# First maxima moved into and behind the projection stage, weights loaded by columns, first y block loaded in halves

## Chip, cores and metric

One core of a Trainium2 chip runs the whole program. The metric is the device time of one execution in microseconds (us), lower is better. The profile is of one further execution; its times are those of the core's own clock, and clock shares are of TensorE's full 2.4 GHz.

## What is computed

The input x is (2, 2048, 512). A conditioned transformer layer is followed by a second layer with a cumulative average. All arithmetic is float32; most products are made three times, with operands split into a high and a low part.

```python
scale, offset = t_emb @ w_scale, t_emb @ w_offset
h = layer_norm(x) * scale + offset
q, k, v = h @ wq / sqrt(512), h @ wk, h @ wv      # 16 heads of 32; q, k then get the rotary embedding
a = softmax(q @ k.T); x = x + (a @ v) @ wo        # 2048 x 2048 logits per batch and head
x = x + gelu(layer_norm(x, s) @ w1) @ w2
# second layer
att = exp((x @ aw - max over the sequence) * temperature)
attn_out = att * cumsum(x @ values) / (att * counts + 1e-30)
op = attn_out @ operator + vector
res = relu(concat([x, op]) @ ff1 + b1) @ ff2 + b2 + x
out = layer_norm(res) * gamma + beta
```

## The kernel before

The program is a chain of stages, each one block of five instruction streams (PE, DVE, ACT, POOL, SP) that wait for each other by semaphores. A stage ends when all its streams are done, and the next begins after its semaphores have been cleared. All results between stages go through DRAM. The order of work in every stream is written out by hand.

**Projection stage** (`prepare`, L81 to L429). Eight blocks n of 512 tokens, four per batch. SP loads x, the conditioning weights (`wa`, `wb`), the joint qkv weight in four chunks of 128 rows (`load_w`, L133) and the rotary table. DVE takes the mean and variance and makes `x_norm` (L282); PE turns it (`turn`, L188), ACT makes h and its high part (`affine`, L353 on), DVE the low part (L289). The qkv weight is split by ACT (L384) and DVE (L317) into a staging buffer of two slots. PE then makes per block eight projections of q and k (L215, 12 matmuls each) and four of v (L224). A q or k projection is rotated by DVE (L303, L305) and POOL (L424), split by ACT (L368) and POOL (L412) and stored by SP (L167), from buffers of four slots. Six PSUM banks go round among the projections. In block 1 there is a small product for the bias (L231, through `vectors`), from `ff1`.

**First maxima** (`first_maxima`, L784 to L911). The softmax needs the row maximum of each block of logits before its scores. For the first 16 row groups (4 heads by 4 groups of 128 queries), and for three groups of the next block, this stage makes them: 76 matmuls of 96 x 512 (L866), each reduced by DVE (L888); PE turns the collected maxima (L876), DVE copies them (L897), SP writes them as a row of the stacked queries (L830). SP first loads queries and keys head by head (`load_head`, L810 on), six DMAs for each of q and k. Beside this PE makes a product of two weights, `operator` by half of `ff1`, as 32 matmul steps (L851), which ACT copies (L906) and SP stores as `wp` (L834). POOL sets a row of ones (L910).

**Attention** (`attend`). 512 steps, 16 key blocks by 4 query blocks by 4 head groups by 2 batches. A step has four score matmuls (L577), four maxima matmuls of a later block (L603), exponentials (ACT, L725), and values (L625). The sum over keys is made by POOL (`POOL_ROUNDS`: step offset and key block added; pairs are first added by DMA, L758) and for key blocks 8 and 14 by PE (L636); `last_sums` (L644) waits for POOL's last round and ends on PE. ACT copies values (L732) and sums (L738), SP stores them.

**Feed-forward** (`feed_forward`). SP loads the sums of all of attention (L1070), DVE takes the reciprocal (L1332), SP stores it as `rl` (L1077). A block of 512 tokens is projected in four parts of 128 (`project`, L1163): SP loads y (L1042) and, as four broadcast DMAs, the reciprocals (L1045) into one buffer, POOL multiplies (L1386), ACT and DVE split (L1222, L1280), PE projects, DVE adds x and takes statistics (L1287, L1289). For the first block nothing else is there for PE; for later ones this is mixed into the up and down products. `load_y` of a part waits for the split of the part before.

**Average** (`average`) is not touched.

## Time and profile before

| | us |
|---|---|
| median of 3 runs (range) | 3707.03 (3705.38 to 3714.58) |
| the profiled execution's own time | 3699.31 |
| its span | 3697.5 |
| PE busy in the span | 3452.5 (93%) |
| mean granted clock | 0.966 |

The span is divided by stage: the first PE work on projections is at 43 us and the last ends at 336 us; the first maxima run from 343 to 422 us; attention from 425 to 2120 us; feed-forward from 2123 us; the average takes the last 600 us or so. A row of the timeline gives start and duration of a run of like instructions, engine, line, operation, output and inputs, how many, and in brackets the idle time before with what ended it. "SPq" and "POOLq" are DMA issues or the engine's sequencer.

### The profile page before, as it was taken

To read this page: it belongs to the slowest core of one execution; us is meant where nothing else is said; L and a number is where in the kernel's file an instruction comes from. 1 tells how busy PE (TensorE), PEld (TensorE's weight loads), DVE (VectorE), ACT (ScalarE), POOL (GpSimd) and SP (SyncE) were. 2 spreads that over 40 slices of the span, in tenths; PEclk is the share of its full clock that TensorE was granted. 3 is DMA by queue.
4 is the path that set the end of the run, shared out by engine and by line. 5 is a ranking of instruction groups with operands and counts; after the bars stand their busy time and mean duration, and the time that the engine had idled before them with its cause. 6 is when DMAs were issued, how large, how long until landed. Compare 5 with 4: busy or idle time off the path is not lost. (4 is left out here: it accounts for less than half of the span.)

```text
span 3697.5 us, 47212 instructions
## 1 busy us (share of the span) xinstructions
PE 3452.5 (93%) x16640; PEld 2256.5 (61%) x16640; DVE 2039.8 (55%) x3300; ACT 1517.4 (41%) x2793; POOL 2109.3 (57%) x1675
## 2 busy tenths in 40 slices
PE   7997899999999999999999759999999995999997
PEld 5775445555554545455455248888888874777776
DVE  5764777777777777777777134222222213434443
ACT  2332366666666666666666522111111112221121
POOL 2655188888988888788888812222222213544553
PEclk9998999999999999999999869999999997999999
DMA  5646686868777786967765443122222114212220
GB/s 184 186 147 183 124 150 120 156 132 153 145 129 148 136 145 120 153 136 136 146 126 109 102 129 105 54 80 66 72 72 69 58 38 144 78 61 79 73 77 37
DMA packets 178716, 421.23 MB, mean 114 GB/s; under 512 B 16176, under 2 KB 65840, under 8 KB 153392
## 3 DMA queue, kind: packets, MB, share of 16 engines
q1 hardware_dynamic: 155440, 250.44, 26.4%
q0 software_dynamic: 23040, 167.78, 23.5%
q8 instruction: 131, 2.15, 0.3%
q14 instruction: 105, 0.86, 0.1%
HBM read 163.10 MB, written 87.03 MB: 68 GB/s over the span
## 5 line engine op out<-in xcount | busy, mean ns | idle before, releaser
L682 DVE TENSOR_REDUCE part_max<-ps_att 128x1 f32<-128x512 f32 x1972 | 1226.1, 683 | 384.8 <-PE ps_att L603 384.6
L725 ACT ACTIVATE probs<-ps_att 128x512 f32<-128x512 f32 x2048 | 1063.4, 602 | 524.0 <-PE ps_att L577 461.6
L776 POOL TENSOR_TENSOR prob_sums<-prob_sums,probs 128x512 f32<-128x512 f32 x896 | 1162.8, 1579 | 43.3 <-DMA probs<-probs 43.3
L577 PE MATMUL ps_att<-q_stack,k_stack 97*128 97x512 f32 x2048 | 867.6, 427 | 30.4 <-ACT probs L725 24.1
L603 PE MATMUL ps_att<-k_stack,q_stack 96*128 96x512 f32 x1972 | 784.0, 398 | 0.0
L577 PEld LDWEIGHTS ps_att<-q_stack,k_stack 97*128 97x128 f32 x2048 | 388.6, 190 | 518.8 <-ACT probs L725 365.3
L625 PE MATMUL ps_att<-probs,v_tok 128*32 128x512 f32 x4096 | 549.3, 608 | 0.0
L1381 POOL TENSOR_TENSOR ff_g_lo<-ff_g,ff_g_hi 128x512 fp32r<-128x512 f32 x128 | 165.1, 1290 | 555.8 <-DVE ff_g_hi L1345 555.8
L603 PEld LDWEIGHTS ps_att<-k_stack,q_stack 96*128 96x128 f32 x1972 | 377.1, 191 | 68.2
L1251 ACT ACTIVATE ff_g<-ps_ff 128x512 f32<-128x512 f32 x128 | 76.6, 599 | 580.6 <-PE ps_ff L1135 580.6
L758 POOL DMA_DIRECT2D probs<-probs x160 | 153.5, 959 | 257.0 <-PE ps_att L625 242.1
L1815 POOL TENSOR_TENSOR av_gated_lo<-av_full,av_gated_hi 128x512 fp32r<-128x512 f32 x64 | 93.3, 1459 | 270.0 <-ACT av_gated_hi L1668 270.0
L1345 DVE CAST ff_g_hi<-ff_g 128x512 fp32r<-128x512 f32 x128 | 54.9, 429 | 304.3 <-ACT ff_g L1251 304.3
L776 POOL TENSOR_TENSOR prob_sums<-probs 128x512 f32<-128x512 f32 x128 | 165.4, 1448 | 47.6 <-DMA probs<-probs 47.6
L625 PEld LDWEIGHTS ps_att<-probs,v_tok 128*32 128x32 f32 x4096 | 80.8, 108 | 182.7 <-ACT probs L725 175.2
L424 POOL TENSOR_TENSOR rotated<-rot_a,rot_b 128x512 f32<-128x512 f32 x64 | 92.4, 1443 | 154.7 <-DVE rot_b L305 149.5
L1668 ACT ACTIVATE av_gated_hi<-av_full 128x512 fp32r<-128x512 f32 x64 | 40.5, 632 | 263.7 <-DVE av_full L1776 263.7
L1135 PE MATMUL ps_ff<-ff_h_hi,w_hi 128*128 128x512 f32 x512 | 143.3, 402 | 0.7 <-ACT ff_h_hi L1263 0.7
L1776 DVE TENSOR_TENSOR av_full<-ps_avg,av_gate_rows 128x512 f32<-128x512 f32 x64 | 44.2, 691 | 177.1 <-PE ps_avg L1562 139.0
L1150 PE MATMUL ps_ff<-w_hi,ff_g_hi 128*128 128x512 f32 x512 | 141.5, 398 | 0.0
L1135 PE MATMUL ps_ff<-ff_h_hi,w_lo 128*128 128x512 f32 x512 | 141.0, 397 | 0.0
L1135 PE MATMUL ps_ff<-ff_h_lo,w_hi 128*128 128x512 f32 x512 | 140.7, 396 | 0.0
(183 smaller groups left out, 4648.0 us busy)
## 6 DMA issues: line engine op xcount, KB each, us to landing
probs<-probs POOLq DMA_DIRECT2D x160, 1024.0 KB, 8.5
q_stack<-qk SPq DMA_DIRECT2D x186, 128.0 KB, 7.3
k_stack<-qk SPq DMA_DIRECT2D x42, 512.0 KB, 11.0
qk<-rot_hi SPq DMA_DIRECT2D x64, 256.0 KB, 4.1
qk<-rot_lo SPq DMA_DIRECT2D x64, 256.0 KB, 2.6
av_gate_rows<-gate SPq DMA_DIRECT2D x64, 256.0 KB
x_in_sb<-in_x SPq DMA_DIRECT2D x8, 1024.0 KB, 8.7
v<-v_stage SPq DMA_DIRECT2D x8, 1024.0 KB, 5.1
```

The source lines that it names most:

```text
L424: nc.gpsimd.tensor_tensor(rot[:, u % 2, :], ra[:, u % 2, :], rb[:, u % 2, :], ALU.add)\
L577: nc.tensor.matmul(sT[u % 3], t["kS"][0:S3 + 1, b, h, k * P:(k + 1) * P], t["qS"][0:S3 + 1, h, n * TB:(n + 1) * TB], start=True, stop=True)\
L603: nc.tensor.matmul(mx[mx_uses % 3], t["qS"][0:S3, h, n * TB + q * P:n * TB + (q + 1) * P], t["kS"][0:S3, b, h, k * TB:(k + 1) * TB], start ...
L625: mm = nc.tensor.matmul(o_ps[rows, :], t["v"][:, steps[w]["b"], k, rows], t["p"][:, w % PR, h, :], start=(k == 0), stop=(k == LT - 1))
L682: nc.vector.tensor_reduce(t["pm"][:, r, k:k + 1], mx[mx_uses % 3], AX.X, ALU.max)\
L725: nc.scalar.activation(t["p"][:, at % PR, h, :], sT[(at * G + h) % 3], ACT.Exp)\
L758: nc.gpsimd.dma_start(t["p"][:, w % PR], t["p"][:, (w + 1) % PR], accum_op=ALU.add).then_inc(sem, 16)
L776: nc.gpsimd.tensor_tensor(x, first, t["p"][:, w % PR, h, :], ALU.add).then_inc(s["acc_done"], 1)
L1135: mm = nc.tensor.matmul(ps[:, 4 + u % 2, :], w[:, f, m * P:(m + 1) * P], h[:, f, :], start=(i == 0 and f == 0), stop=(i == 2 and f == DC - 1))
L1150: mm = nc.tensor.matmul(ps[:, j, :], g[:, u % 2, j * P:(j + 1) * P], w[:, m, :], start=(m == 0 and i == 0), stop=(m == MC - 1 and i == 2))
L1381: nc.gpsimd.tensor_tensor(gl[:, u % 2, :], gf[:], gh[:, u % 2, :].bitcast(F32), ALU.subtract)\
L1815: nc.gpsimd.tensor_tensor(al[:, v % 2, :], af[:, v % 2, :], ah[:, v % 2, :].bitcast(F32), ALU.subtract).then_inc(s["a_lo"], 1)
```

## The change

Five edits, all in the four functions named:

1. The 76 maxima of `first_maxima` move into `prepare`. From block 5 (`MAX_FROM`) one maxima matmul follows each of the twelve projections of a block, 36 in all, with its reduction on DVE; the other 40 come behind the last projection, each with a step of the weight product while there are any. The maxima share the ring of six banks. Heads are loaded by SP among the stores of blocks 4 to 6, three DMAs of 32 rows each in place of six of 16. The bias product goes from block 1 to behind the last block. `first_maxima` is gone; queries 1 and 2 and the values of the first unit are now loaded at the start of attention, and the row of ones is set in two parts.
2. The qkv weight is loaded by columns (q, k, v) in three DMAs of 1 MB; the projections go through all q first, then k; x is normed in place; the loads of x move.
3. In the last block of attention PE adds key blocks 8, 11, 12, 13, 14, 15 and POOL five rounds in place of eight.
4. The reciprocals of batch 0 are made inside attention, those of batch 1 in block 0 of feed-forward (`AT_RECIP`).
5. The first block of y and its reciprocals come in two halves of 256 tokens into the idle buffers of h (`load_first`).

```diff
+LAST_SUMS = (8, 11, 12, 13, 14, 15)
+LAST_ROUNDS = tuple(x for x in POOL_ROUNDS if x[1] not in LAST_SUMS)
...
+MAX_FROM = 5
...
+        rh, rl = sb("rot_hi", [P, 4, TB]), sb("rot_lo", [P, 4, TB])
+        wa, wb = rh, rl
...
+        raw = vst[:].rearrange("p a g j n -> p a (g j n)").rearrange("p a (f n) -> p a f n", f=DC)
+        op = x[:].rearrange("p a j f -> p (a j f)").rearrange("p (k n) -> p k n", k=DC)
+        ff, q1 = hf, hl[:, 0, 0, :]
+        kept = vst[:, 0].rearrange("p g j n -> p (g j n)").rearrange("p (i n) -> p i n", i=4)
+        pieces = [(i, slice(i * D, (i + 1) * D), slice(f, f + 2), float(D) ** -0.5 if i == 0 else 1.0)
+                  for i in range(3) for f in (0, 2)]
...
-        uses = []
+        uses, early = [], 0
         for n in range(NA):
-            uses += [("qk", n * QK + i) for i in range(QK)] + [("v", n * TT + j) for j in range(TT)]
-            if n == 1:
-                uses += [("b1", 0)]
+            for kind, first, count in (("qk", n * QK, QK), ("v", n * TT, TT)):
+                for i in range(count):
+                    uses += [(kind, first + i)]
+                    if n >= MAX_FROM:
+                        uses += [("mx", early)]
+                        early += 1
+        uses += [("b1", 0)]
+        for m in range(early, TT * AHEAD):
+            uses += [("mx", m)]
+            if m == TT * JOBS + TT - 1:
+                uses += [("mt", 0)]
...
                 def load_x(n):
                     if n >= 2:
-                        sp.wait_ge(s["xn"], TT * (n - 1))
+                        sp.wait_ge(s["turned"], DC * (n - 1))
                     sp.dma_start(x[:, n % 2], x_v[n]).then_inc(s[f"x_in{n % 2}"], 16)
 
...
+                def load_w(i):
+                    if i >= 2:
+                        sp.wait_ge(s["w_lo"], 2 * (i - 1))
+                    sp.dma_start(raw[:, i % 2], a["wqkv"][:, :, i * D:(i + 1) * D]).then_inc(s[f"wq_in{i % 2}"], 16)
...
                 sp.dma_start(wb[:], a["w_offset"]).then_inc(s["w_in"], 16)
+                load_w(0)
+                load_tab(0, TB, "tab_in0")
                 load_w(1)
-                load_tab(0, TB, "tab_in0")
...
+                def load_head(which, h):
+                    dst = (t["q0"], t["k0"])[which][:, h, :]
+                    if which == 0 and h == 0:
+                        for i in range(4):
+                            sp.wait_ge(s[f"st_h{i}"], 16 * QK * NB // 4)
+                            sp.wait_ge(s[f"st_l{i}"], 16 * QK * NB // 4)
+                    for part, hl_at in enumerate(((0, 1, 0), (0, 0, 1))[which]):
+                        src = a["qk"][which, 0, hl_at, 0:P, 0:dst.shape[-1]].rearrange("(a r) t -> a r t", a=2)
+                        sp.dma_start(dst[part * KD:(part + 1) * KD].bitcast(F32), src[:, h * HD:(h + 1) * HD, :])\
+                            .then_inc(s[f"head_in{h}"], 16)
+
                 load_x(1)
+                load_tab(TB, L, "tab_in1")
                 load_x(2)
...
+                        if i == 5 and n + 3 < NA:
+                            load_x(n + 3)
+                        if n >= NB and i % 3 == 1 and (n - NB) * 3 + i // 3 < 2 * G:
+                            m = (n - NB) * 3 + i // 3
+                            load_head(m % 2, m // 2)
+                        if n == NA - 1 and i == 2:
+                            sp.wait_ge(s["turned"], DC * NA)
+                            sp.dma_start(op, a["opT"]).then_inc(s["op_in"], 16)
+                            sp.wait_ge(s["lo"], DC * NA)
+                            sp.dma_start(ff[:], a["ff1"][:, DC:2 * DC, :]).then_inc(s["b_in"], 16)
+                            sp.dma_start(b1[:], a["ff1_bias"]).then_inc(s["b_in"], 16)
+                        if n == NA - 1 and i == 3:
+                            wait_done(sp, "v", n * TT - 1)
+                            for part, hl_at in enumerate((0, 1, 0)):
+                                src = a["qk"][0, 0, hl_at, 0:P, TB:2 * TB].rearrange("(a r) t -> a r t", a=2)[:, 0:HD, :]
+                                sp.dma_start(q1[part * KD:(part + 1) * KD].bitcast(F32), src).then_inc(s["q1_in"], 16)
                         for hl_at, sem, done, src in ((0, f"st_h{u % 4}", "rhi", rh), (1, f"st_l{u % 4}", "rlo", rl)):
                             sp.wait_ge(s[done], u + 1)
...
+                for i in range(HC):
+                    if i == HC // 2:
+                        sp.wait_ge(s["mt_out"], 1)
+                        for h in range(G):
+                            sp.dma_start(t["q0"][S3:S3 + 1, h, :].bitcast(F32).rearrange("a (j p) -> a j p", p=P),
+                                         t["mT"][h * TT:(h + 1) * TT, 0, :].bitcast(F32)).then_inc(s["max_set"], 16)
+                    sp.wait_ge(s["wp_out"], i + 1)
+                    sp.dma_start(a["wp"][:, i, :], kept[:, i % 4, :]).then_inc(s[f"wp_stored{i % 4}"], 16)
...
+                def maxima(m):
+                    j, key = m // TT, m % TT
+                    h, rows = j // TT % G, slice(j % TT * P, (j % TT + 1) * P)
+                    if j % TT == 0 and key == 0 and j < JOBS:
+                        pe.wait_ge(s[f"head_in{h}"], 16 * 6)
+                    if j == JOBS and key == 0:
+                        pe.wait_ge(s["q1_in"], 16 * 3)
+                    wait_bank("mx", m)
+                    q = t["q0"][0:S3, h, rows] if j < JOBS else q1[0:S3, rows]
+                    nc.tensor.matmul(bank("mx", m), q, t["k0"][0:S3, h, key * TB:(key + 1) * TB], start=True, stop=True)\
+                        .then_inc(s["mm"], 1)
...
+                def product(i, f):
+                    if i == 0 and f == 0:
+                        pe.wait_ge(s["op_in"], 16)
+                    if i >= 2 and f == 0:
+                        pe.wait_ge(s["wp_out"], i - 1)
+                    mm = nc.tensor.matmul(ps[:, i % 2, :], op[:, f, i * P:(i + 1) * P], ff[:, f, :],
+                                          start=(f == 0), stop=(f == DC - 1))
+                    if f == DC - 1:
+                        mm.then_inc(s["wp_mm"], 1)
...
+                        if n >= MAX_FROM:
+                            maxima(m)
+                            m += 1
...
+                wait_bank("b1", 0)
+                pe.wait_ge(s["b_in"], 32)
+                for f in range(DC):
+                    mm = vectors(bank("b1", 0)[:, f * B:(f + 1) * B], ff, f)
+                mm.then_inc(s["mm"], 1)
+                for r, m in enumerate(range(m, TT * AHEAD)):
+                    maxima(m)
+                    if m == TT * JOBS + TT - 1:
+                        turn_maxima()
+                    if r < HC * DC:
+                        product(r // DC, r % DC)
...
+                def keep_max(m):
+                    j, key = m // TT, m % TT
+                    wait_done(dve, "mx", m)
+                    if j == JOBS and key == 0:
+                        dve.wait_ge(s["neg_max"], 1)
+                    nc.vector.tensor_reduce(t["pm"][:, j % JOBS, key:key + 1], bank("mx", m), AX.X, ALU.max)\
+                        .then_inc(s["mx_free"], 1)
+                    if m == TT * JOBS - 1:
+                        dve.wait_ge(s["mx_free"], TT * JOBS)
+                        nc.vector.tensor_reduce(t["nm"][:, 0, :], t["pm"][:], AX.X, ALU.max, negate=True)\
+                            .then_inc(s["neg_max"], 1)
...
+                weight_lo(0)
+                weight_lo(1)
+                for u in range(2, len(pieces)):
+                    weight_lo(u)
...
+                act.wait_ge(s["vec_out"], 2)
+                affine(0, 0)
+                affine(0, 1)
+                weight_hi(0)
+                weight_hi(1)
                 affine(0, 2)
                 affine(0, 3)
+                for u in range(2, len(pieces)):
+                    weight_hi(u)
...
+                act.wait_ge(s["st_v0"], 16 * NA // 2)
+                for i in range(HC):
+                    act.wait_ge(s["wp_mm"], i + 1)
+                    if i >= 4:
+                        act.wait_ge(s[f"wp_stored{i % 4}"], 16 * (i // 4))
+                    nc.scalar.activation(kept[:, i % 4, :], ps[:, i % 2, :], ACT.Copy).then_inc(s["wp_out"], 1)
...
+    def shares(n):
+        return (LAST_SUMS, LAST_ROUNDS) if n == blocks - 1 else (PE_SUMS, POOL_ROUNDS)
...
+            load_q(0, 0, 1, "q_first1")
+            sp.dma_start(t["v"][:, 0].rearrange("p k n -> p (k n)"), a["v"][0, 0:P, :]).then_inc(s["v_first"], 16)
+            load_q(0, 0, 2, "q_first2")
...
+                if at == end - 18:
+                    sp.wait_ge(s["l_stored"], 16 * (blocks - 3))
+                    sp.wait_ge(s["pv"], (UNITS - 1) * STEPS)
+                    sp.dma_start(sums0[:, 0, :], a["lS"][:, 0:L].rearrange("h (c t) -> h c t", t=TB)).then_inc(s["l_in"], 16)
+                if at == end - 9:
+                    sp.wait_ge(s["recip"], 1)
+                    sp.dma_start(a["rl"][:, 0:L].rearrange("h (c t) -> h c t", t=TB), sums0[:, 1, :]).then_inc(s["rl_stored"], 16)
...
+                    pe.wait_ge(s[f"q_first{n}"], STACK)
...
+                if w == 0:
+                    pe.wait_ge(s["v_first"], 16)
...
             values(end - 1)
+            sums(end - 1)
             last_sums(blocks - 1)
...
+                if at == end - 12:
+                    dve.wait_ge(s["l_in"], 16)
+                    nc.vector.reciprocal(sums0[:, 1, :], sums0[:, 0, :]).then_inc(s["recip"], 1)
...
+            nc.gpsimd.memset(t["k1"][S3:S3 + 1].bitcast(F32), 1.0).then_inc(s["ones_set"], 1)
+            pool.wait_ge(s["ones_set"], 1)
...
-def first_maxima(nc, c, a, s, t, ps):
...
+                def load_first(half):
+                    cols = slice(half * 2 * P, (half + 1) * 2 * P)
+                    sp.dma_start(hh[:, :, cols].bitcast(F32), y_v[:, :, cols]).then_inc(s[f"y_first{half}"], 16)
+                    for f in range(DC):
+                        src = a["rl"][f * G:(f + 1) * G, cols].unsqueeze(1).broadcast_to([G, KD, 2 * P])
+                        sp.dma_start(hl[:, f, cols].bitcast(F32), src).then_inc(s[f"y_first{half}"], 16)
...
                 for i in range(4):
                     load_chunk(i)
+                load_first(0)
                 load_x(0)
-                sp.wait_ge(s["recip"], 1)
-                sp.dma_start(r_v, one_over).then_inc(s["rl_stored"], 16)
+                load_first(1)
                 for i in range(4, 8):
                     load_chunk(i)
-                sp.wait_ge(s["rl_stored"], 16)
-                load_y(0, 0)
+                sp.dma_start(sums1, l_v).then_inc(s["l_in"], 16)
...
+                        if m == AT_RECIP and n == 0:
+                            sp.wait_ge(s["recip"], 1)
+                            sp.dma_start(r_v, sums1).then_inc(s["rl_stored"], 16)
...
+                                cols = slice(j * P, (j + 1) * P)
+                                pool.wait_ge(s[f"y_first{j // 2}"], 16 * (DC + 1))
+                                if v:
+                                    pool.wait_ge(s["y_lo"], v)
+                                nc.gpsimd.tensor_tensor(yr[:], hh[:, :, cols].bitcast(F32), hl[:, :, cols].bitcast(F32),
+                                                        ALU.mult).then_inc(s["y_n"], 1)
```

## Rows read from the trace of the kernel before

**Rows 1.** Windows: us, five engines (count), granted clock, DMA share, GB/s
```profile
10.00:15.00 5.00, 1.85 (x10) 1.88 (x10) 2.64 (x10) 1.67 (x3) 0.00 (x0) 1.00 1.01 422
...
340.00:425.00 85.00, 55.45 (x141) 29.50 (x141) 48.63 (x78) 4.78 (x8) 13.75 (x1) 0.76 0.67 142
...
380.00:400.00 20.00, 20.00 (x62) 11.33 (x61) 19.32 (x31) 1.79 (x3) 0.00 (x0) 1.00 0.76 131
...
2139.00:2143.00 4.00, 0.00 (x0) 0.00 (x0) 0.00 (x0) 0.00 (x0) 0.00 (x0) 0.50 0.16 47
```

**Rows 2.** Timeline, last projections to first maxima
```profile
334.27 1.10 PE L224 MATMUL ps_pre<-qkv_lo,h_hi 128*128 128x512 f32 x4
...
335.20 1.09 PE L224 MATMUL ps_pre<-qkv_hi,h_lo 128*128 128x512 f32 x4
...
336.95 0.37 SPq L169 DMA_DIRECT2D v<-v_stage  x1
...
353.72 8.35 PE L866 MATMUL ps_att<-k_stack,q_stack 96*128 96x512 f32 x14 [17.43 <-DMA k_stack<-qk]
```

**Rows 3.** Timeline of the maxima and the weight product
```profile
401.44 1.02 PE L851 MATMUL ps_att<-probs 128*128 128x512 f32 x2
...
402.78 1.02 PE L851 MATMUL ps_att<-probs 128*128 128x512 f32 x2
...
408.13 0.27 DVE L897 CAST max_turned<-ps_att 16x128 fp32r<-16x128 f32 x1
...
408.43 2.68 SPq L830 DMA_DIRECT2D q_stack<-max_turned  x4
...
411.15 10.64 SPq L834 DMA_DIRECT2D wp<-probs  x8
```

**Rows 4.** Timeline of the start of attention
```profile
425.14 3.17 SPq L487 DMA_DIRECT2D q_stack<-qk  x6
...
425.74 0.63 PE L603 MATMUL ps_att<-k_stack,q_stack 96*128 96x512 f32 x1
```

**Rows 5.** DMA issues, 424 to 432 us: KB each, us to landing
```profile
q_stack<-qk SPq DMA_DIRECT2D x6, 128.0 KB, 4.4
```

**Rows 6.** Timeline of PE in block 1, the bias product
```profile
118.75 3.63 PE L231 MATMUL ps_pre<-cond,pre_wa 128*128 128x2 f32 x32
```

**Rows 7.** Timeline of the start of the projection stage
```profile
28.84 0.78 ACT L356 ACTIVATE h_full<-ps_pre,offset_all,scale_all 128x512 f32<-128x512 f32 x1 [11.07 <-DVE offset_all L313]
...
43.18 2.08 PE L215 MATMUL ps_pre<-h_hi,qkv_hi 128*128 128x512 f32 x4 [11.00 <-ACT h_hi L361]
...
48.23 1.92 DVE L282 TENSOR_SCALAR x_norm<-x_in_sb,x_mv,x_rstd 128x512 f32<-128x512 f32 x4
...
62.48 0.63 PE L194 MATMUL ps_pre<-ident,x_norm 128*128 128x128 f32 x4 [1.10 <-ACT h_full L356]
```

**Rows 8.** Timeline of the end of attention
```profile
2101.60 15.21 POOL L776 TENSOR_TENSOR prob_sums<-prob_sums,probs 128x512 f32<-128x512 f32 x12
...
2103.19 1.04 PE L636 MATMUL ps_att<-probs,ones 128*32 128x512 f32 x8
...
2104.05 1.04 PE L625 MATMUL ps_att<-probs,v_tok 128*32 128x512 f32 x8
...
2116.87 1.94 PE L644 MATMUL ps_att<-prob_sums,ones 128*32 128x512 f32 x8 [11.78 <-POOL prob_sums L776]
```

**Rows 9.** Timeline of the start of feed-forward
```profile
2122.96 0.32 SPq L1070 DMA_DIRECT2D ff_g<-lS  x1
...
2135.17 0.38 SPq L1042 DMA_DIRECT2D ff_y<-yT  x1
...
2143.94 1.26 POOL L1386 TENSOR_TENSOR ff_y<-ff_y,ff_rl 128x512 f32<-128x512 f32 x1 [27.13 <-DMA ff_rl<-rl]
...
2145.92 2.07 PE L1163 MATMUL ps_ff<-wo_hi,ff_y_hi 128*128 128x512 f32 x4 [27.12 <-ACT ff_y_hi L1222]
...
2185.88 0.69 DVE L1287 TENSOR_TENSOR ff_x<-ps_ff,ff_x 128x512 f32<-128x512 f32 x1 [4.20 <-PE ps_ff L1163]
```

340 lines of the change are left out of this document (124 added, 216 removed).

## The prediction

> **What bounds the kernel now.** I first read the windows by stage. In attention, feed-forward and most of the projection stage PE hardly stops, and the change leaves those streams as they are; so I looked for windows where PE stands or runs at a low granted clock. There are three, and the change touches all three.
>
> The first is from 340 to 425 us: PE busy 55.45 of 85 us at a granted clock of 0.76 [rows 1]. The timeline shows why. The last projection ends at 336.3 us, a 1 MB store follows, and the first maxima matmul starts at 353.72 after 17.43 us without PE, the last wait being for keys [rows 2]. Then two maxima and one product step take 1.34 us, which is DVE's pace of two reductions (two maxima and two product instructions at 0.235 us would be 0.94). SP ends the stage with four maxima DMAs and eight `wp` stores [rows 3]. Attention's first own maxima matmul is at 425.74 [rows 4].
>
> The second is the end of attention: PE waits 11.78 us for POOL's last adds before `last_sums` [rows 8]. The third is the start of feed-forward: its first DMA is at 2122.96, the first y part is multiplied at 2143.94, PE starts at 2145.92, and the fourth part is projected only at 2185.88 [rows 9]. So four projections take 40 us, though twelve matmuls at 0.235 us (0.93 us for four, [rows 2]) are 2.8 us each. The reader is to see in every row of rows 9 that the releaser is the chain DMA, POOL, ACT, PE: one load at a time.
>
> **Part 1, the maxima.** Before, from the last projection's end to the first maxima matmul of attention: 425.74 - 336.29 = 89.4 us [rows 2, 4]. After, the same stretch holds:
> - the bias product, moved here: 3.6 us [rows 6];
> - 32 pairs of maxima and product step. DVE needs 0.67 us for one, PE 3 x 0.235 = 0.7 us: PE and DVE are level, I take 0.69, so 22 us; the turning and copy add 0.5;
> - SP's tail: it waits for the turned maxima before the second half of the `wp` stores, so 2.7 us for four DMAs [rows 3] and 4 x 0.4 for four stores, 4.3 us in all. The last eight maxima (5.4 us of DVE) run beside this and beside the landing;
> - last store issued to the next stage's first issue: 425.14 - 421.79 = 3.35 us [rows 3, 4];
> - new: attention now loads queries 1 itself, before its first maxima. Six DMAs at 0.44 to 0.53 us of issue, the last landing 4.4 us later [rows 4, 5]: 6.8 us. The 1 MB of values behind them is first needed two steps later and is hidden; the queries 2 and 3 behind that, twelve more issues on SP, are needed twelve steps later and are hidden too. The first key load of the next unit waits behind them, without a reader for 60 steps.
>
> Sum 3.6 + 22.5 + 4.3 + 3.35 + 6.8 = 40.6 us, so 48.8 us less.
>
> The projection stage grows. On PE 36 maxima at 0.235 us are 8.5 us. On DVE each costs 0.67 us beside 2.1 us of rotation, 2.8 us in a pair where PE needs 3.05, so DVE stays below PE; if this cover were gone, the price would be 36 x 0.67 less 8.5, 16 us. The bank ring still lets PE lead by three projections. The bias product leaves: -3.6 us. The eight head loads (24 DMAs, some 11 us of SP issue among stores that leave SP mostly idle) cost nothing by issue, but see below: I put 2 us for stores held up. The loads of `operator` and `ff1`, 3 MB at 422 GB/s [rows 1] or 7.5 us of DMA, stand ahead of three or four stores in the last block; the four-slot buffer covers 12 us. So 6.9 us more; net of part 1: 42 us less.
>
> The row of ones: POOL's 16,384 elements were set beside SP's loads. Half is now set at the start of the projections, when POOL idles, and half at the start of attention, while PE waits for the queries: nothing. If not covered it would cost 7 us.
>
> **Part 2, weights by columns.** Before, the first projection waits 11 us for h and starts at 43.18, since ACT stands waiting for weight chunks [rows 7]. After, ACT does h from 28.84 (four times 1.4 us) and two halves of the q weight (2.1 us), so PE starts at about 36.6, 6.6 us earlier. But the path is not PE. The third weight load is released only by the split of the first, at about 35 us, and the x of block 1 is queued behind it; at 422 GB/s both are in by 42 us [rows 1]. DVE splits the last weight to 43, then statistics and x of block 1 (before, these end at 50.15, [rows 7]): now about 48.4. PE makes two projections, then waits there for the turn. Before, PE waits again at 62.48 on the chain from DVE through POOL and ACT [rows 7]; this chain starts 1.7 us earlier. So 6.6 us become 0 to 1.7; I take 1. Bounds: a loss of 2 if the clock falls in the new 4 us wait, a gain of 3.
>
> **Part 3, sums.** PE adds four key blocks more. One costs 2104.05 - 2103.19 = 0.86 us [rows 8]. Three come inside steps (2.6 us), one behind the last values. So `last_sums` can start at 2103.2 + 2.6 + 3 x 0.86, about 2108, where it was 2116.87. POOL keeps five rounds. Of the twelve adds that ran from 2101.60 to 2116.8 [rows 8] four are left; even started no earlier they take 15.21 / 3 = 5.1 us and end at 2106.7, in time. `last_sums` also runs at the full clock, 1 us in place of 2. Copy, store and stage change are as before: 9.5 us less.
>
> **Part 4, reciprocals.** The 2.7 us load, 3.35 us reciprocal and store of batch 0 fall behind steps in which DVE has no maxima. SP's wait at 9 steps before the end has only one store of sums behind it. The second half costs DVE 3.35 us in block 0, beside two weight splits in a 5.6 us step of PE: DVE is full for one step, I take 0.5 us (0 to 3).
>
> **Part 5, y in halves.** Before, 23.0 us from the stage's first DMA to PE [rows 9]. After: two small and four weight loads, 6 x 0.53 = 3.2 us of issue, then the y half. Before, from y's issue to POOL was 2143.94 - 2135.17 = 8.8 us, and to PE 2 us more. So PE starts at 3.2 + 8.8 + 2.0 = 14.0. Its first projection is at half clock, 5.6 us. The next need no DMA: from the end of a projection DVE adds x, takes statistics, splits a weight and y, 4 x 0.69 = 2.8 us, then PE's last four matmuls take 1, so 4.0 us each. Sum 14.0 + 5.6 + 12 = 31.6 in place of 2185.88 - 2122.96 = 62.9: 31 us less. Were the clock low throughout, a projection would set the pace with 6.2 us: 25 us less. With 0.94 us of matmuls in every 1.34 us, as from 380 to 400 us, the granted clock stayed at 1.00 [rows 1], and 2.8 in 4.0 is the same share, so I stay near the better end: 30 us less.
>
> The halves have rows of 1 KB in place of 512 B. What this costs shows in a window after the last broadcast issue: 47 GB/s, 0.16 of the engines [rows 1], while elsewhere all move 422. So these loads run on about 3 of 16 engines, 13 to 18 GB/s each against 26, limited by pieces rather than bytes; the same number of pieces takes about as long. If it went by bytes, +5 us for the first half.
>
> The Trainium skill ("DMA: Bandwidth & Descriptors", section "Why a DMA increments its semaphore by 16 and not by 1") says that a DMA is spread over the largest number of engines, up to 16, that divides the outermost size of both sides. By that rule, the broadcast of 4 rows uses four; the trace agrees with its 0.16.
>
> **Sum.** 42 + 1 + 9.5 - 0.5 + 30 = 82 us. The profiled execution took 3699.3 us, so 3617.3; it is 7.7 us under the median of the runs, so the median becomes 3625 us.
>
> **The rivals.**
> - *A: head loads hold up the stores.* The heads now come as two groups of 16 rows. A DMA that spreads as narrowly as the broadcast, at 47 GB/s [rows 1], needs 16.7 us for a head's keys (768 KB). A store queued behind lands so late that the four-slot buffer (14 us) runs out, ACT and then PE stand. Two of the four key loads have the v projections behind them as cover (12 us); the others cost 7 us each, and with x loads behind them 20 in all: 3640. Against it: keys have pieces of 8 KB. By the skill's rule (same page and section) these loads get two engines, a head's keys take 15 us, and this rival is the likely one; the six-DMA form in use now gets sixteen. Chance 0.2.
> - *B: the front of feed-forward gives less*, by bytes or clock as above, or since weight chunks behind the halves land late: 20 us in place of 30, 3635. Chance 0.15.
> - *C: the maxima are not hidden*, since DVE is late in the bank ring: 16 us more, 3641. For it: DVE would be at 90% in those blocks. Chance 0.07.
> - *D: slower.* The mechanism of A at its worst: the broadcast had four rows outermost and moved 47 GB/s [rows 1]; if the rate goes with that count whatever the pieces, the heads' two groups move 24 GB/s, and a head's keys take 32 us, four times, with all stores and x loads behind. Above 82 us of stall, or 20 us for each head, all is lost; here each stalls 32 + 5 - 14 = 23 us, 92 us: 3717. Against it the 422 GB/s of all sixteen, 26 each, with large pieces [rows 1]. Chance 0.05.
> - *E: it doesn't take effect*: attention's start waits so long for queries and values, behind stores of 1 MB and 2 MB, that the gain of part 1 goes there: 3660. Chance 0.03.
>
> **The numbers.** The forecast has 0.5. Its own range is 3612 to 3638. With A, B and C the range of 8 in 10 is 3604 to 3656. A measurement tells some 0.3%, 11 us, from no change. Faster 0.93 (all but D and part of E), same 0.02, slower 0.05.
>
> **What would show it.** Right: the last projection ends near 343 us and attention's first maxima matmul is near 383; pairs of maxima and product at 0.7 us; `last_sums` 4 us after the last values; PE's first projection in feed-forward 14 us after its first DMA, the others 4 us apart at full clock. Wrong: in A, ACT idle before its rotated high part, released by a DMA store, in blocks 5 and 6; in C, PE idle behind DVE there; in B, PE waiting in feed-forward for a weight or for POOL released by DMA. The step of attention (3.06 us) should be the same.

## The result, and the profile after

The changed kernel took 3655.47 us (median; 3647.95 to 3659.54), the kernel before, run beside it on the same chip, 3710.81 us (3705.38 to 3716.28). The ratio is 0.9854, with a 95% interval of 0.9829 to 0.9878: 55 us or 1.5% less, where the forecast said 82. The profiled execution took 3653.45 us with a span of 3651.7, which is 45.8 less than the profiled span of before. The forecast of 3625 was 30 us too low, and its own range ended at 3638; the measured median lies at the upper end of the range that the rivals widen, 3604 to 3656.

Step by step, from the profile after. First the last projections and the maxima behind them. This is the timeline (start, duration, engine, line, operation, how many, idle time before and what ended it).

```profile
347.23 3.63 PE L283 MATMUL ps_pre<-cond,h_full 128*128 128x2 f32 x32
...
371.75 0.80 PE L296 MATMUL ps_pre<-k_first,q_first 96*128 96x512 f32 x1
372.39 1.02 PE L309 MATMUL ps_pre<-h_full,x_in_sb 128*128 128x512 f32 x2
372.85 0.80 PE L296 MATMUL ps_pre<-k_first,q_first 96*128 96x512 f32 x1
...
387.41 0.27 DVE L455 CAST max_turned<-ps_pre 16x128 fp32r<-16x128 f32 x1
387.71 2.53 SPq L215 DMA_DIRECT2D q_first<-max_turned  x4
390.28 1.90 SPq L218 DMA_DIRECT2D wp<-v_stage  x4
```

The bias product, which follows the last projection at once, begins at 347.23, where some 342 to 343 were forecast. Then a maxima matmul and a product step come every 1.10 us (371.75 to 372.85), not every 0.69. The four maxima DMAs and four stores behind the turned maxima are as foreseen [rows 3]. The windows of these stretches (us, PE, PEld, DVE, ACT and POOL busy with counts, granted clock, DMA share, GB/s), to be read beside [rows 1]:

```profile
350.86:387.40 36.54, 36.54 (x98) 18.77 (x98) 22.44 (x34) 4.19 (x7) 0.00 (x0) 0.95 0.10 36
387.40:396.04 8.64, 2.44 (x9) 1.32 (x8) 5.16 (x10) 0.61 (x2) 0.01 (x1) 0.78 0.33 122
396.04:404.12 8.08, 0.77 (x2) 0.29 (x2) 0.00 (x0) 1.87 (x2) 6.91 (x1) 0.50 0.80 158
```

Between the bias product and the turned maxima PE is busy for all of 36.54 us and DVE for 22.44: PE sets that pace. The granted clock is 0.66 in the first 5 us of it and 1.00 behind. Behind it come 8.64 us of tail and stage change and 8.08 of waiting, at the end of which the clock is at half.

Next the start of attention, same view:

```profile
396.07 0.77 PE L735 MATMUL ps_att<-q_first,k_first 97*128 97x512 f32 x1 [6.23 <-PEq L57]
...
398.75 0.43 SPq L663 DMA_DIRECT2D v_tok<-v  x1
399.22 6.04 SPq L631 DMA_DIRECT2D q_stack<-qk  x12
404.12 0.80 PE L763 MATMUL ps_att<-k_first,q_stack 96*128 96x512 f32 x1 [7.28 <-DMA q_stack<-qk]
...
411.87 1.01 POOL L924 DMA_DIRECT2D probs<-probs  x1 [8.91 <-PE ps_att L787]
...
432.43 4.93 POOL L942 TENSOR_TENSOR prob_sums<-probs 128x512 f32<-128x512 f32 x4 [10.52 <-DMA probs<-probs]
...
433.72 0.60 ACT L891 ACTIVATE probs<-ps_att 128x512 f32<-128x512 f32 x1 [4.61 <-POOL prob_sums L942]
```

PE waits 8.05 us (396.07 to 404.12) for queries 1; then PE is in step until ACT stands for POOL, whose first add had to wait for a paired copy (the DMA that adds one block of probabilities to another) issued at 411.87. Attention's first maxima matmul is at 404.12 in place of 425.74 [rows 4], 21.6 us earlier. The forecast had 383.

The end of attention and the front of feed-forward:

```profile
2095.62 1.04 PE L787 MATMUL ps_att<-probs,v_tok 128*32 128x512 f32 x8
2096.48 1.04 PE L798 MATMUL ps_att<-probs,ones 128*32 128x512 f32 x8
2097.34 1.04 PE L806 MATMUL ps_att<-prob_sums,ones 128*32 128x512 f32 x8
...
2102.60 0.34 SPq L1120 DMA_DIRECT2D ln_scale_sb<-in_ln_scale  x1
...
2105.85 4.19 SPq L1084 DMA_DIRECT2D ff_h_lo<-rl  x4
...
2113.28 8.04 SPq L1084 DMA_DIRECT2D ff_h_lo<-rl  x4
...
2118.82 1.26 POOL L1446 TENSOR_TENSOR ff_y<-ff_h_hi,ff_h_lo 128x512 f32<-128x512 f32 x1 [25.50 <-DMA ff_h_lo<-rl]
...
2120.80 2.07 PE L1214 MATMUL ps_ff<-wo_hi,ff_y_hi 128*128 128x512 f32 x4 [22.42 <-ACT ff_y_hi L1273]
...
2121.36 2.87 SPq L1072 DMA_DIRECT2D ff_z<-in_w  x4
...
2129.73 1.38 ACT L1267 ACTIVATE w_hi<-ff_z,ln_scale_sb 128x512 fp32r<-128x512 f32 x2 [8.99 <-DMA ff_z<-in_w]
...
2131.69 2.08 PE L1214 MATMUL ps_ff<-wo_hi,ff_y_hi 128*128 128x512 f32 x4 [5.40 <-ACT ff_y_hi L1273]
...
2145.15 0.69 DVE L1338 TENSOR_TENSOR ff_x<-ps_ff,ff_x 128x512 f32<-128x512 f32 x1 [1.06 <-PE ps_ff L1214]
```

The wait of 11.78 us for POOL [rows 8] is gone: `last_sums` runs straight behind the last values and sums. In feed-forward the fourth add of x comes 42.55 us after the stage's first DMA (2102.60 to 2145.15), against 62.9 before [rows 9] and 31.6 in the forecast. The four narrow broadcasts of the second half hold SP for 8.04 us, so the weight chunks 4 to 7 are issued at 2121.36, and ACT stands 8.99 us before them.

To compare runs I cut each profile at the same events. "First score" is the first PE work of attention, "maxima" its first maxima matmul; "first block" goes from there to the first store of values; "body" from that store to the last but one; "end" from there to feed-forward's first DMA; "front" from there to the fourth add of x. All are us of one profiled execution. Behind the front, to the end of the span, it is 1505.9 to 1515.1 us in all fourteen.

| run | bias product | first score | maxima | first block | body | end | front | span |
|---|---|---|---|---|---|---|---|---|
| before | | 425.17 | 425.74 | 57.1 | 1579.1 | 61.0 | 62.9 | 3697.5 |
| before, again | | 429.32 | 429.89 | 57.1 | 1587.1 | 61.0 | 62.3 | 3705.2 |
| b1_sums | | 426.18 | 426.74 | 57.0 | 1590.3 | 51.6 | 61.7 | 3701.4 |
| changed | 347.23 | 396.07 | 404.12 | 64.6 | 1582.2 | 51.7 | 42.6 | 3651.7 |
| changed, again | 346.80 | 395.65 | 403.41 | 59.6 | 1589.8 | 51.7 | 42.0 | 3661.6 |
| e1_heads16 | 341.43 | 388.58 | 396.67 | 63.7 | 1585.4 | 51.7 | 43.1 | 3653.6 |
| e2_deferq | 348.32 | 395.48 | 403.55 | 59.1 | 1585.2 | 51.7 | 43.3 | 3653.1 |
| e3_spread | 349.00 | 396.16 | 404.29 | 60.1 | 1584.2 | 51.7 | 37.9 | 3644.1 |
| e4_order | 347.66 | 394.83 | 402.92 | 63.3 | 1579.9 | 51.6 | 40.4 | 3646.6 |
| e5_noprod | 347.88 | 381.71 | 389.53 | 56.7 | 1587.5 | 51.7 | 43.2 | 3636.0 |
| e7_max8 | 338.26 | 411.27 | 419.44 | 59.5 | 1586.5 | 51.7 | 42.0 | 3668.8 |
| e8_q1kept | 348.07 | 396.92 | 397.48 | 64.8 | 1582.3 | 51.7 | 43.2 | 3649.5 |
| c1_all | 340.79 | 391.38 | 391.95 | 59.7 | 1582.7 | 51.8 | 32.8 | 3629.5 |
| c2_early | 341.67 | 390.68 | 391.25 | 58.1 | 1589.8 | 51.7 | 32.6 | 3632.6 |

### The profile page after: what moved, and what is told of

The parts are those of the page before. It is cut to its first block and busy times, and to the rows that moved or that the text cites. A ratio compares the mean times of both kernels' runs of the same rounds, so it can differ in the third digit from the quotient of the medians.

```text
span 3651.7 us, 47181 instructions
## 1 busy us (share of the span) xinstructions
PE 3451.7 (95%) x16672; PEld 2252.2 (62%) x16672; DVE 2051.3 (56%) x3299; ACT 1515.4 (41%) x2791; POOL 2095.9 (57%) x1663
## 5 line engine op out<-in xcount | busy, mean ns | idle before, releaser
L942 POOL TENSOR_TENSOR prob_sums<-prob_sums,probs 128x512 f32<-128x512 f32 x884 | 1146.9, 1562 | 61.8 <-DMA probs<-probs 61.8
L735 PE MATMUL ps_att<-q_stack,k_first 97*128 97x512 f32 x768 | 328.0, 427 | 14.1 <-ACT probs L891 14.0
L735 PE MATMUL ps_att<-q_stack,k_stack 97*128 97x512 f32 x768 | 321.4, 427 | 10.6 <-ACT probs L891 10.0
L763 PE MATMUL ps_att<-k_first,q_stack 96*128 96x512 f32 x756 | 304.6, 403 | 7.3 <-DMA q_stack<-qk 7.3
L763 PE MATMUL ps_att<-k_stack,q_stack 96*128 96x512 f32 x768 | 303.7, 395 | 0.0
L735 PEld LDWEIGHTS ps_att<-q_stack,k_first 97*128 97x128 f32 x768 | 146.5, 191 | 199.4 <-ACT probs L891 141.3
L735 PEld LDWEIGHTS ps_att<-q_stack,k_stack 97*128 97x128 f32 x768 | 143.7, 189 | 199.1 <-ACT probs L891 146.6
L763 PEld LDWEIGHTS ps_att<-k_first,q_stack 96*128 96x128 f32 x756 | 146.3, 194 | 34.3 <-DMA q_stack<-qk 7.8
L763 PEld LDWEIGHTS ps_att<-k_stack,q_stack 96*128 96x128 f32 x768 | 145.7, 190 | 26.3
```

The costliest lines, as they stand in the source:

```text
L735: nc.tensor.matmul(sT[u % 3], kS[b][0:S3 + 1, h, k * P:(k + 1) * P], q_rows(n)[0:S3 + 1, h, :], start=True, stop=True)\
L763: nc.tensor.matmul(mx[mx_uses % 3], q_rows(n)[0:S3, h, q * P:(q + 1) * P], kS[b][0:S3, h, k * TB:(k + 1) * TB], start=True, stop=True).the ...
L942: nc.gpsimd.tensor_tensor(x, first, t["p"][:, w % PR, h, :], ALU.add).then_inc(s["acc_done"], 1)
```

## The experiments

Four theories came out of the comparison: narrow head loads hold the projections up; a product step costs PE more than I took; the narrow broadcasts and the order behind them delay the front; loads in flight at attention's start delay POOL's copies. All edits but b1_sums are made to the changed kernel.

**e1_heads16**, the head loads in the form of the kernel before:

```
-    src = a["qk"][which, 0, hl_at, 0:P, 0:dst.shape[-1]].rearrange("(a r) t -> a r t", a=2)
-    sp.dma_start(dst[part * KD:(part + 1) * KD].bitcast(F32), src[:, h * HD:(h + 1) * HD, :])\
-        .then_inc(s[f"head_in{h}"], 16)
+    for half in range(2):
+        row, at = half * 64 + h * HD, part * KD + half * HD
+        src = a["qk"][which, 0, hl_at, row:row + HD, 0:dst.shape[-1]]
+        sp.dma_start(dst[at:at + HD].bitcast(F32), src).then_inc(s[f"head_in{h}"], 16)
```

> The changed kernel with each head load as six DMAs of 16 rows in place of three of two groups (48 DMAs in place of 24). Theory (few engines: a DMA whose outer size is two is carried by two engines, so a head's rows come late and SP's own issue is held, 8.98 us at the worst): the first keys land within 8 us of their issue, PE's wait of 4.12 us before the first maxima matmul goes, no SP issue over 2 us, the last projection ends 3 to 5 us earlier (342 to 344 in place of 347). Rival (the wait is the maxima's own work, or the bank ring): the projections end at 346 to 348 as now. Second rival (SP's issue of 24 more DMAs is what costs): they end later than 347.

SP's issues and PE's wait (timeline), first in the changed kernel:

```profile
213.75 1.86 SPq L177 DMA_DIRECT2D k_first<-qk  x3
...
217.78 8.98 SPq L207 DMA_DIRECT2D qk<-rot_hi  x1
...
234.85 0.55 PE L296 MATMUL ps_pre<-k_first,q_first 96*128 96x512 f32 x1 [4.12 <-DMA k_first<-qk]
```

and in e1_heads16:

```profile
213.86 3.40 SPq L179 DMA_DIRECT2D k_first<-qk  x6
...
218.79 0.56 SPq L208 DMA_DIRECT2D qk<-rot_hi  x1
```

One store behind the narrow loads took SP 8.98 us to issue; behind the wide ones it is 0.56. A store issued just behind the narrow ones, at 215.66, landed 19.8 us later; behind the wide ones it was 6.2. PE's wait of 4.12 us is gone, and so is the half clock that followed it from 235.20 to 238.60. The bias product begins at 341.43, 5.8 us earlier, where 3 to 5 were expected. Block 5 of the projections took 44.67 us in the changed kernel and 38.75 here, counted from the last matmul of one block to that of the next.

Attention's first score comes 7.5 us earlier, but 1.7 of it is not the head loads. In the changed kernel the clock was low just behind the bias product, 0.66 over 5 us, and in e1_heads16 it was not; from the bias product to the first score it took 48.84 and 47.15 us. The same stretch was 47.15 to 47.17 in e2, e3 and e4, where the clock did not fall, and 48.85 in the second profile of the changed kernel, where it did.

So the cause named in rival A was at work, but by another path. Its sign was there: ACT waited 8 times for a store of `rot_hi` in the changed kernel, 32.4 us in all, and once, 6.2 us, in e1_heads16 (170 to 348 us). PE did not stand behind ACT, though; it stood once, for the keys of the maxima themselves. That is why the price was smaller than 20 us. Median 3651.37, ratio 0.9829 (0.9804 to 0.9854): against the changed kernel's ratio this alone can't be told apart, since the body varies by more (see below).

By the Trainium skill ("DMA: Bandwidth & Descriptors", section "Why a DMA increments its semaphore by 16 and not by 1") a DMA uses the largest number of engines, up to 16, that divides the slowest dimension of both sides. By that rule the narrow loads use two, and the trace of the changed kernel agrees: while SP is held, the DMA share (last but one) is 0.12, two of sixteen. In e1_heads16 it is 1.04 from 214.5 to 224.5 us.

```profile
224.50:226.50 2.00, 2.00 (x10) 1.62 (x9) 0.00 (x0) 0.60 (x1) 0.00 (x0) 1.00 0.12 49
```

**e5_noprod**, the products left out (`wp` is not computed; one matmul of 8 columns stands in for the four steps of each output tile):

```
-    if r < HC * DC:
-        product(r // DC, r % DC)
+    if r < HC:
+        nc.tensor.matmul(ps[:, r % 2, 0:8], op[:, 0, 0:P], ff[:, 0, 0:8], start=True, stop=True)\
+            .then_inc(s["wp_mm"], 1)
```

> The changed kernel without the products of operator and ff1 (wp is left out: one small matmul per output tile stands in for four products, so the product and its result are not computed). Theory (a product step is two instructions of 0.43 us on PE, so PE sets the 1.09 us of a pair): the maxima behind the projections are 0.67 to 0.70 us apart, DVE's pace, and from the bias product to the turned maxima 10 to 14 us less than in the changed kernel. Rival (the copies and stores of wp on ACT and SP, or DVE, set the pace): they stay 1 us apart.

In its timeline of the same place, DVE now sets the pace with five reductions in 3.07 us, and PE runs ahead of it:

```profile
359.45 3.07 DVE L406 TENSOR_REDUCE part_max<-ps_pre 128x1 f32<-128x512 f32 x5
359.71 2.76 PE L296 MATMUL ps_pre<-k_first,q_first 96*128 96x512 f32 x6
...
373.05 0.27 DVE L459 CAST max_turned<-ps_pre 16x128 fp32r<-16x128 f32 x1
```

From the bias product to the turned maxima it is 25.2 us (347.88 to 373.05) in place of 40.2 (347.23 to 387.41): 15 us, one more than the 10 to 14 expected. Attention's first score is 14.4 us earlier. The maxima are not 0.67 to 0.70 us apart, as expected, but 0.61 in the lines above: DVE is faster than both the forecast and this expectation had it. ACT's copies and SP's stores stayed as many as they were and only PE's work shrank, so the rival that names them is out. The term that I sized at PE's 0.7 us is PE's, but 1.10. The time of the one execution was 3637.81 us.

**e7_max8**, no maxima among the projections:

```
-MAX_FROM = 5
+MAX_FROM = 8
```

> The changed kernel with no maxima among the projections: all 76 stand behind them (head loads as before). Theory (PE pays a maxima matmul wherever it stands, 0.235 us, and DVE's time is hidden in the projections but not behind them): the projections end 8 to 9 us earlier, the tail has 32 pairs at 1.09 us and 44 maxima at DVE's 0.67 us more or, where they lie beside products, a pace of 1.33 us for two and a product; so the tail grows by 36 x 0.67 = 24 us less the slack that PE's product steps leave DVE (32 x 0.42 = 13), 11 to 24 us, and attention starts 2 to 16 us later. Rival (maxima inside the projections cost PE more than 0.235 each, by bank waits): attention starts earlier than now or at the same time.

The bias product in e7_max8, and DVE behind the last product step (timeline):

```profile
338.26 4.46 PE L283 MATMUL ps_pre<-cond,h_full 128*128 128x2 f32 x32 [2.40 <-DMA b_in<-in_ff_bias]
...
380.63 19.23 DVE L402 TENSOR_REDUCE part_max<-ps_pre 128x1 f32<-128x512 f32 x32 [0.40 <-PE ps_pre L296]
```

It begins 9.0 us earlier (338.26 against 347.23) though it waits 2.40 us for its bias, so the projections end 11.4 us earlier, not 8 to 9; the maxima's own wait for the narrow head loads left with them. Attention starts 15.2 us later (411.27 against 396.07): from the bias product to the first score it is 73.0 us against 48.8, 24.2 more. Where DVE has nothing but maxima it makes 32 in 19.23 us, 0.60 each, so 36 of them are 21.6 us; the other 2.6 are a bias product that took 4.46 us in place of 3.63 and a longer stretch at low clock behind it. Median 3665.67, ratio 0.9876 (0.9853 to 0.9898). The first theory holds at its upper end. Its sentence that PE's product steps leave DVE 13 us of slack did not come true: behind the last step DVE had all the others left to do. Moving the maxima was worth 15 us in the profile.

**e8_q1kept**, queries 1 loaded once, in the first stage, into a tile that attention keeps (it takes the place of one half of `h_lo`, which is free by then):

```
-    load_q(0, 0, 1, "q_first1")
...
+    q1=first("q_second", [P, DC, TB], F32R),
```

> The changed kernel with queries 1 of all heads loaded once in the first stage into a tile that attention keeps, so attention loads only values and queries 2 and 3 at its start. Theory (attention's start is bound by that load, 8.05 us, and by the low clock that follows it, 4 us at half clock): PE's first maxima matmul is 0.5 to 1 us after the stage's first score, the first values step waits for v_tok instead, 2 to 4 us, and the stage gains 4 to 7 us up to its first store of values. Rival (the values, 1 MB, land as late as the queries did): the wait only changes its name, gain 0 to 2 us.

The start of attention in e8_q1kept (timeline):

```profile
397.48 0.63 PE L765 MATMUL ps_att<-k_first,q_second 96*128 96x512 f32 x1
...
404.35 1.01 POOL L926 DMA_DIRECT2D probs<-probs  x1 [0.55 <-POOL k_stack L946]
...
427.88 4.94 POOL L944 TENSOR_TENSOR prob_sums<-probs 128x512 f32<-128x512 f32 x4 [13.51 <-DMA probs<-probs]
...
429.17 0.60 ACT L893 ACTIVATE probs<-ps_att 128x512 f32<-128x512 f32 x1 [7.59 <-POOL prob_sums L944]
```

PE's first maxima matmul follows 0.56 us behind the first score (396.92), and PE did not wait for `v_tok`, where 2 to 4 us were expected. But POOL's first add came 23.5 us after its copy was issued, ACT stood 7.59 us for it, and PE 6.1 us for ACT. The first values are stored 65.4 us after the first score, 72.7 and 67.4 in the two profiles of the changed kernel: 7.3 and 2.0 less, so the 4 to 7 expected are not shown. The wait was taken away and a part of it came back one engine further on. Median 3651.48, ratio 0.9834 (0.9817 to 0.9851).

**e2_deferq**, queries 2 and 3 of the first unit loaded later:

```
-    load_q(0, 0, 2, "q_first2")
...
+    if unit == 0 and w in (7, 15):
+        sp.wait_ge(s["score"], G * w)
+        load_q(0, 0, *((2, "q_first2") if w == 7 else (NB - 1,)))
```

> The changed kernel with queries 2 and 3 of the first unit loaded at steps 7 and 15 of attention instead of ahead of step 0. Theory (contention: twelve loads of 128 KB in flight make POOL's paired copies land 18.3 us after issue instead of 9, so POOL's first adds start at 432 and ACT waits 4.6 us for a slot of probs): the first paired copy lands within 10 us, POOL's first add starts 20 us or less after the first maxima matmul (28.3 now, 17.9 before), the ACT wait for POOL in the first block is under 1 us, and the first block (first maxima matmul to first store of values) takes about 57 us as before the change, not 64.6. Rival (POOL's queue is slow at a stage start by itself): the block stays at 62 to 65 us.

POOL and ACT in e2_deferq (timeline):

```profile
411.02 1.01 POOL L927 DMA_DIRECT2D probs<-probs  x1 [8.67 <-PE ps_att L790]
...
421.12 4.99 POOL L945 TENSOR_TENSOR prob_sums<-probs 128x512 f32<-128x512 f32 x4
...
449.95 0.60 ACT L894 ACTIVATE probs<-ps_att 128x512 f32<-128x512 f32 x1 [2.29 <-POOL prob_sums L945]
...
479.68 0.60 ACT L894 ACTIVATE probs<-ps_att 128x512 f32<-128x512 f32 x1 [9.81 <-POOL prob_sums L945]
```

The first add starts 17.6 us behind the first maxima matmul, with no wait for the copy; in the changed kernel it was 28.3. In the eight profiles with the loads ahead it was 21 to 30, and the add came 13.9 to 23.5 us after the issue of its copy. In the three with the loads deferred, and in the three of the old order, it was 17 to 18, and 10.1 us after the issue. So the loads in flight do delay the copy. But the expectation of 57 us for the block and no ACT wait failed: ACT waits for POOL at 450 and 480 us. The block took 59.1 here, 59.7 and 58.1 in the combinations, against 56.7 to 64.8, 61.5 in the mean, in the eight others. The means differ by some 2.5 us, but the three lie inside the range of the eight, so a gain is not shown. What delays POOL's later copies stays open. The median, 3660.11, ratio 0.9862 (0.9844 to 0.988), shows no gain either.

**e3_spread**, the same bytes in as many broadcasts, laid out by head:

```
-    for f in range(DC):
-        src = a["rl"][f * G:(f + 1) * G, cols].unsqueeze(1).broadcast_to([G, KD, 2 * P])
-        sp.dma_start(hl[:, f, cols].bitcast(F32), src)
+    for h in range(G):
+        src = a["rl"][h::G, cols].unsqueeze(0).broadcast_to([KD, DC, 2 * P])
+        sp.dma_start(hl[h * KD:(h + 1) * KD, :, cols].bitcast(F32), src)
```

> The changed kernel with the reciprocals of the first y block broadcast by one DMA for each head (32 rows outermost, four feature chunks inside) in place of one for each feature chunk (4 heads outermost); as many DMAs and bytes. Theory (the outer size sets the engines: 4 before, 16 now): in feed-forward's front SP's issue of the second four takes 2 us in place of 8.04, the first y half reaches POOL 4 us or more earlier (12 us after the stage's first DMA in place of 16.2), the weight chunks behind come 6 us earlier, and DVE's fourth add of x is at 33 to 38 us after the stage's start in place of 42.6. Rival (time goes by pieces or bytes whatever the engines): issue stays at 8 us, the add at 42 to 43.

Its front (timeline):

```profile
2100.28 0.35 SPq L1120 DMA_DIRECT2D ln_scale_sb<-in_ln_scale  x1
...
2107.42 4.26 SPq L1084 DMA_DIRECT2D ff_h_lo<-rl  x4
2111.73 2.28 SPq L1072 DMA_DIRECT2D ff_z<-in_w  x4
...
2113.37 1.26 POOL L1446 TENSOR_TENSOR ff_y<-ff_h_hi,ff_h_lo 128x512 f32<-128x512 f32 x1 [22.53 <-DMA ff_h_lo<-rl]
```

The issue of the second four fell from 8.04 to 4.26 us (2 expected), POOL began 13.1 us after the stage's first DMA in place of 16.2, the chunks were issued 7.3 us earlier against that start, and the front took 37.9 in place of 42.6, inside the 33 to 38 expected. The DMA share was 1.00 from 2105 to 2111 us; in the changed kernel it was 0.27 from 2119 to 2122, where the narrow broadcasts were nearly alone. Median 3645.87, ratio 0.9821 (0.9805 to 0.9838).

**e4_order**, the weight chunks ahead of the second half:

```
-    load_first(1)
     for i in range(4, 8):
         load_chunk(i)
+    load_first(1)
```

> The changed kernel with the weight chunks 4 to 7 of feed-forward issued ahead of the second y half (and nothing else; the reciprocals are broadcast as in the change). Theory (ACT stands in its program behind chunk 4, issued 18.8 us after the stage's first DMA because SP is held 8.04 us by the second half's broadcasts): ACT's wait of 8.99 us for a weight goes, PE's second projection begins 5.6 to 6.5 us after its first in place of 10.9; if the second half lands too late for the third projection, that one waits 1 to 3 us; the fourth add of x comes 37 to 40 us after the stage's start in place of 42.6. Rival (the order only moves the wait from chunk 4 to the second half): 42 to 43 us.

PE in e4_order (timeline):

```profile
2116.14 2.08 PE L1214 MATMUL ps_ff<-wo_hi,ff_y_hi 128*128 128x512 f32 x4 [22.68 <-ACT ff_y_hi L1273]
2122.21 1.20 PE L1214 MATMUL ps_ff<-wo_hi,ff_y_hi 128*128 128x512 f32 x4 [0.79 <-ACT ff_y_hi L1273]
2128.64 2.07 PE L1214 MATMUL ps_ff<-wo_hi,ff_y_hi 128*128 128x512 f32 x4 [3.26 <-ACT ff_y_hi L1273]
```

The second projection follows after 6.07 us, and the third waits 3.26 us for the second half. The front is 40.4, just above the 37 to 40 expected: of the 5 us saved at the second projection, 2.2 are left. Median 3648.64, ratio 0.983 (0.9805 to 0.9855). Order and spread together give 32.8 (c1_all below), more than the sum of the two alone, since each alone leaves the other's wait.

**b1_sums**, the kernel before with part 3 alone (`LAST_SUMS` and `LAST_ROUNDS` for its last block, as in the diff of the change):

> The kernel before with the last block's sums alone moved to PE (six key blocks there, five adds left to POOL), and nothing else. Theory (the part is worth what the last wait was): last_sums begins within 2 us of the last values, the wait of 11.78 us for POOL goes, the end of attention is 8 to 10 us earlier against its last but one store of values, and from the first to the last but one store of values it takes 1579 us as in the profile of before. Rival (the 3 to 6 us that attention's body took longer in all profiles of the changed kernel, 1582 to 1585, are the spread of executions and not of the change): here too the body is 1582 us or longer.

The end of attention took 51.6 us in place of 61.0, 9.4 less, and the body 1590.3. That the body would take 1579 us again failed, and the rival stood: the code of the body is that of before, and it took 11 us longer. Median 3702.37, ratio 0.9976 (0.9954 to 0.9998), which agrees with 9 us and could hold 1 or 17.

**r_before and r_after**, both kernels profiled once more:

> The kernel before, unchanged, profiled a second time. Theory (attention's body, from the first to the last but one store of values, varies by some 11 us from execution to execution, and its 1579.1 us in the profile of before lay at the low end): it is 1582 to 1590 us here, and the span is 3700 to 3712. Rival (the body of before is 1579 by its own layout, and the change made it 3 to 10 us longer): 1577 to 1581 again.

> The changed kernel, unchanged, profiled a second time. Theory (the terms before attention and of feed-forward's front are fixed by the program, the body and the first block are not): the bias product begins at 347 to 349 us, attention's first score at 394.5 to 397, feed-forward's front takes 42 to 43.5 us; the first block takes 57 to 65 us by how late POOL's first copy lands, the body 1580 to 1590 us. Rival (the executions agree in all of it): first block 64.6, body 1582.2, each within 1 us.

The kernel before had a body of 1587.1 this time, 8.0 us more than in the profile that the forecast was made from; its first block, end and front are within 1 us, and its span, 3705.2, is inside the expected range. The changed kernel had a first block of 59.6 and a body of 1589.8; its bias product began at 346.80, just below the expected 347, and its front took 42.0. Over three bodies of the old code (1579.1 to 1590.3) and eleven of the new (1579.9 to 1589.8) the change adds nothing that can be seen there. What makes a body long is not shown. PE waited there for ACT 19.6, 23.5 and 21.9 us in the three of the old code, which is 4 of the 8 us between the first two.

That the terms before attention are fixed by the program failed too. The first score of the kernel before came 4.2 us later than in its first profile, and 3.1 of it arose behind the bias product of block 1. These are the same 5 us in the first and in the second profile (columns as above):

```profile
122.40:127.40 5.00, 5.00 (x22) 4.04 (x23) 2.18 (x4) 0.00 (x0) 0.00 (x0) 1.00 0.02 3
122.40:127.40 5.00, 5.00 (x14) 4.12 (x15) 0.17 (x1) 0.00 (x0) 0.00 (x0) 0.50 0.00 0
```

One program, one place: the clock stayed full in one execution and was at half in the other.

**c1_all**: e1, e2, e3, e4 and e8 in one kernel.

> The changed kernel with the four edits together (head loads in sixteens of rows, queries 1 kept from the first stage, queries 2 and 3 later, reciprocals of the first y block broadcast with 32 rows outermost) and the weight chunks 4 to 7 issued ahead of the second y half. If the gains of the single runs add (head loads 7.5 us at the stage's end, attention's first block 13 to 15 us from queries kept and POOL's copies in time, front of feed-forward 4.6 us and 3 to 5 more from the order): attention starts near 388.5, its first values are stored 57 to 60 us later, feed-forward's fourth add of x comes 33 to 35 us after the stage's start, and the time is 3625 to 3632 us. Rival (attention's steady state is set by POOL and its copies, so that what is gained at its start is given back in the blocks behind): the distance from the first to the last store of values grows to 1634 us or more, and the time is 3640 to 3648.

Median 3633.17 us, ratio 0.9798 (0.9772 to 0.9823), whose interval lies below the changed kernel's (0.9829 to 0.9878): 22 us less than the changed kernel by the medians. It is 1 us above the range of the first theory, and far from the rival's. The front is 32.8, the first values are stored 60.3 us after the first score (72.7 and 67.4 in the two profiles of the changed kernel), the body did not grow. Attention started at 391.4, not 388.5. The windows behind the bias product (columns as above) show why: c1_all runs at half clock there, and from the bias product to the first score it takes 50.6 us, in e1_heads16 47.2. First c1_all:

```profile
345.00:350.00 5.00, 5.00 (x9) 2.65 (x10) 1.55 (x3) 0.00 (x0) 0.00 (x0) 0.50 0.03 9
```

and e1_heads16:

```profile
345.00:350.00 5.00, 5.00 (x15) 2.67 (x15) 3.12 (x6) 0.36 (x1) 0.00 (x0) 1.00 0.14 51
```

**c2_early**, the same with `operator` and `ff1` loaded at the start of the last block:

```
-    if n == NA - 1 and i == 2:
+    if n == NA - 1 and i == 0:
```

> The combined version with operator and ff1 loaded at the start of the last block of projections in place of its third (the rest as in the combined version before). Theory (the low clock of 3 us behind the bias product, 1.09 us of product steps at 2.1 us, comes by chance of when the clock is judged, and ff1 lands in time in both): no gain but for the clock, 3628 to 3633 us median. Rival (the loads compete with the last stores and with queries 1, so that the last stores and PE come late): the projections end 1 us or more earlier and attention starts at 388 to 390 in place of 391.4.

Median 3637.64, ratio 0.9793 (0.9772 to 0.9815): the same as c1_all, and above the 3628 to 3633 expected. The projections did not end earlier (bias product at 341.67, against 340.79), so the rival is not borne out. The clock fell again behind the bias product, 0.66 from 345 to 350. It fell there in both combinations, in both profiles of the changed kernel, and in e5, e7 and e8, and not in e1, e2, e3 or e4. The two profiles of the kernel before, above, show that it can differ between executions of one program. What decides it stays open.

## Why the prediction was wrong in size

The direction was right. The largest step that failed is the price of a pair of maxima and product step: it was put at 0.69 us, with DVE and PE level, and measured 1.10, set by PE alone. Four other terms were too good as well. From forecast to profile, 82 to 45.8 us:

- **The pairs: "PE needs 3 x 0.235 = 0.7 us ... I take 0.69, so 22 us".** A pair took 1.10 us, the stretch to the turned maxima 36.5. Short by 14.0, of which 1.7 are the low clock at its start. The error was in reading rows 1 to 3: 0.235 us is a projection's matmul of the rounded type; a product step is a full float32 one, recorded as two instructions, and 1.10 less a maxima matmul of 0.235 leaves 0.86 us for it. With 2 x 0.235 + 0.86 = 1.33 the old 1.34 us was PE's pace. I wrote it down as DVE's, "DVE's pace of two reductions", but DVE alone makes two in 1.2 us: 32 in 19.23 us in e7_max8, and 14 maxima in 8.35 us before there were products beside them [rows 2]. PE busy for 20.00 of 20 us from 380 to 400 [rows 1] said the same.
- **The head loads: "I put 2 us for stores held up", rival A at 20.** 5.9 us by e1_heads16. Short by 3.9. The cause is rival A's, the path is not: PE stood once, for keys, and not behind ACT. The prediction calls this rival "the likely one" and still gives it 0.2, and 2 us in the sum; the two do not go together.
- **SP's tail and the queries: 7.65 and 6.8 us.** 8.6 (387.41 to 396.04) and 8.05. Short by 2.2.
- **"The queries 2 and 3 behind that ... are hidden too."** They are for PE, not for POOL's copies, which they delay (e2_deferq). The first block took 64.6 in place of 57.1: 7.5 in that profile; 4.4 in the mean of the eight. This cost stood in no rival.
- **The front: "PE starts at 3.2 + 8.8 + 2.0 = 14.0", then 5.6 and 4.0 each.** PE started at 18.2 (e3: 3.1 us of it by the narrow broadcasts), and the second projection came 10.9 us after the first, since ACT stood for a weight. The third came 5.97 us behind it: the second projection had run at a clock of 0.72 (2133 to 2139 us), and the clock was full only from 2139 on. "2.8 in 4.0 is the same share, so I stay near the better end" was drawn from a row in which PE was busy for all of the time, not for 0.94 in 1.34 us. The fourth, after 4.39, was near 4. Short by 9.6 of 30. Rival B had this mechanism ("weight chunks behind the halves land late: 20 us in place of 30"), and its number was 20.4.
- **Part 2, 1 us.** The first projection began at 36.79 (36.6 forecast), and then PE waited for x of block 1, as described, 6.32 us; that turn began at 50.67, 0.8 us earlier than before. But the clock was at 0.79 from 43.0 to 50.6 and at 0.81 from there to 60 us, where it had been full. The last matmul of block 0 began at 82.83 us, 0.5 later than the 82.35 of before. So the part gained nothing, short by 1.5, inside the bounds given ("a loss of 2 if the clock falls").
- **Part 3, 9.5 us.** 9.4 in b1_sums, 9.3 in the changed kernel.
- **The maxima among the projections, 8.5 us.** 8.0: blocks 5 to 7 took 38.75, 38.17 and 36.37 us in e1_heads16, 36.18, 35.42 and 33.68 before. Rival C, DVE in the bank ring, was not seen: from 260 to 340 us PE was busy for all 80, here and in the changed kernel.
- **Rival D** needed 32 us for a head's keys; PE had them 21 us after the first issue (213.75 to 234.85), and only once too late. Rival E's late start of attention was 8 us, not 35.

The shortfalls are 14.0 + 3.9 + 2.2 + 7.5 + 9.6 + 1.5 = 38.7 us, and 3.1 for the body and 0.2 for part 3. Against them stand 0.5 for the maxima, the 0.5 that was set down for the reciprocals, and 5.1 behind the front (1506.5 against 1511.6 to the end), where the reciprocals' own cost can't be told from the spread of 9 us. That leaves 35.9, and the forecast missed the profiled span by 36.2.

**The baseline.** The median gained 55 and the profiled span 46. The profiled execution of before was 11.5 us under the median of its runs, that of the changed kernel 2.0 under its own; a body at the low end of its spread is most of it. The forecast took its gain off the profiled time and added 7.7 us to come to the median, which is the same as 3707 less 82. Of the 30 us by which it missed the median, the gain was short by 27 (82 against 55); the other 3 to 4 are the 3707 that it started from, against 3710.8. Since the sum above is made against one profile, some of its terms hold luck: the 3.1 of the body, the 5.1 behind the front and, of the 7.5, the 3 by which the first block was above its mean.

## What to carry to other kernels

Before a pace is put down to one engine, look for a stretch where it works alone, and add up what the other does in the same period from durations of those very instructions. Here DVE's own pace was 0.60 us for a reduction, as 14 maxima in 8.35 us had shown [rows 2], and the 0.67 taken for it was PE's: 36 maxima fewer freed 0.235 us each and not 0.67. A load that "no one needs for long" still occupies DMA engines that an on-path copy shares; ask what else is in flight, not only who reads it. And lay a DMA out with 16 or 32 rows outermost, as here, where it would have two or four: the narrow one delays everything issued behind it, and SP with it.

## What the runs showed of the hardware

- A DMA issue on SP is not a fixed 0.4 us: behind three narrow loads of keys one store took 8.98 us to issue, behind six wide ones 0.56, and four narrow broadcasts took 8.04 us, where as many wide ones took 4.26. While the narrow loads held SP, the DMA share was 0.12.
- A reduction of 128 x 512 on DVE is recorded with 0.69 us, but back to back they come every 0.60 us (32 in 19.23).
- The same program's attention body took 1579.1 and 1587.1 us in two executions; the changed one 1582.2 and 1589.8. The stretch before attention differed by 4.2 us in the first pair. One profile is no baseline for terms under 10 us.
- The clock fell to half during or behind a bias product of 32 matmuls of two columns, though PE was busy for all of it, in 7 of 11 profiles of the changed code and in one of three of the old code: in c1_all 5.00 of 5 us at 0.50, and the next product step 2.14 us behind the last (345.63 to 347.77) in place of 1.10.
